# A mixture-of-experts tail: the last six prefetches of result rows are put behind the wait for all expert results

## The reference

```python
mod = (_silu(L0_c) @ L0_wmod).reshape(4, 6, 1, -1)
sa, ca, ga, sb, cb, gb = (mod[:, n] for n in range(6))   # ga, gb kept at least 0.25 away from zero
h = _layernorm(x) * (1 + ca) + sa
x = x + ga * attention(h)        # 16 heads, 4 sink keys and a window of 128 keys
h = _layernorm(x) * (1 + cb) + sb
x = x + gb * moe(h)
# moe: scores = sigmoid(h @ gate_w.T); the best 2 of 16 experts, their weights scaled to sum to 2.5
#   routed = sum over the two of weight * (silu(h @ w_gate[e]) * (h @ w_up[e])) @ w_down[e]
#   shared = (silu(h @ ws_gate) * (h @ ws_up)) @ ws_down
#   result = routed + shared
```

## Time and profile before

| | |
|---|---|
| time, median of 3 runs | 348.93 us (348.56 to 351.56) |
| span of the profiled execution | 347.5 us, first to last instruction |
| own time of the profiled execution | not listed apart; the median of the runs stands 1.43 us above its span |
| busy: PE / DVE / POOL / ACT | 80% / 67% / 59% / 47% of the span |
| DMA | 59.80 MB, mean 172 GB/s over the span |

### The profile page before, as it was taken

How to read it: one execution, slowest core, us unless ns; L and a number is a source line. 1 busy time by engine, 2 the same in 40 slices (tenths; PEclk the granted TensorE clock), 3 DMA queues, 4 the chain that set the end, 5 groups by cost and what they waited for, 6 DMA issues and landing times.

```text
span 347.5 us, 6287 instructions
## 1 busy us (share of the span) xinstructions
PE 278.8 (80%) x1665; PEld 215.0 (62%) x1666; DVE 231.3 (67%) x899; ACT 162.2 (47%) x518; POOL 205.2 (59%) x254
## 2 busy tenths in 40 slices
PE   4897889998988899989774999898899898886000
PEld 3264457656766576757543989787788787775000
DVE  0477477998889886997885645544345477763990
ACT  3142562278225822556222455454545566654550
POOL 3713116738784777558557356564655578875981
PEclk9996996999899996999988799999999999999555
DMA  7949001133624649702286644454456778869793
GB/s 261 330 132 347 16 2 49 59 100 115 197 80 135 183 127 320 163 30 93 72 228 205 201 138 121 144 177 133 138 160 180 245 210 254 263 188 343 247 360 139
DMA packets 41438, 59.80 MB, mean 172 GB/s; under 512 B 5092, under 2 KB 29880, under 8 KB 41404
## 3 DMA queue, kind: packets, MB, share of 16 engines
q1 hardware_dynamic: 34312, 39.91, 39.4%
q0 software_dynamic: 6528, 17.90, 14.3%
q10 hardware_dynamic: 564, 1.59, 1.4%
HBM read 33.57 MB, written 25.80 MB: 171 GB/s over the span
## 4 chain that ended last, share of the span: by engine, by line
PE 54%; DVE 22%; DMA 7%; issue 7%; ACT 4%; POOL 2%; another core or an unknown queue 1%; SPq 1%; DVEq 0%; POOLq 0%; ACTq 0%
PE bank L1227 16%; PE bank L892 8%; PE bank L1237 8%; PE bank L1085 6%; PE bank L1029 3%; PE bank L1052 3%; DVE bank L1752 3%; PE bank L1105 3%; DMA ht<-in_L_attn_x_dram 2%; PE bank L1067 2%; DVE h_sb L1369 2%; DMA ys<-pt_win,row_i 2%; PE bank L935 1%; PE bank L906 1%; DMA p_win<-slots 1%
## 5 line engine op out<-in xcount | busy, mean ns | idle before, releaser
L648 POOL DMA_INDIRECT ys<-pt_win,row_i x72 | 72.6, 1009 | 51.0 <-ACT pt_win L676 27.5
L1227 PE MATMUL bank<-ht,w_now 128*128 128x128 f32 x576 | 78.3, 280 | 4.4 <-issue 4.4
L593 POOL DMA_INDIRECT slots<-h_sb,slot_i x64 | 63.2, 987 | 30.1 <-issue 15.3
L1227 PEld LDWEIGHTS bank<-ht,w_now 128*128 128x128 f32 x576 | 71.7, 195 | 5.4 <-issue 5.1
L1741 DVE TENSOR_TENSOR act_t<-bank,sg 128x128 f32<-128x128 f32 x72 | 20.9, 290 | 48.5 <-ACT sg L843 33.2
L676 ACT ACTIVATE ht<-bank 128x256 f32<-128x256 f32 x104 | 39.9, 383 | 22.5 <-PE bank L892 15.6
L1237 PE MATMUL bank<-w_dn,act_t 128*128 x144 | 44.8, 393 | 5.4 <-DVE act_t L1741 4.3
L676 ACT ACTIVATE pt_win<-bank 128x256 f32<-128x256 f32 (+1 forms) x88 | 37.2, 423 | 21.7 <-PE bank L1237 9.6
L1085 PE MATMUL bank<-w_route,ht 128*128 128x272 f32 x128 | 41.5, 452 | 5.5 <-ACT ht L676 3.2
L892 PE MATMUL bank<-ident,p_win 128*128 128x128 f32 x198 | 36.1, 278 | 4.9 <-issue 3.2
L843 ACT ACTIVATE sg<-bank 128x128 f32<-128x128 f32 x72 | 20.1, 279 | 42.2 <-PE bank L1227 29.6
(11 more groups left out here) (260 smaller groups left out, 489.2 us busy)
## 6 DMA issues: line engine op xcount, KB each, us to landing
p_win<-slots SPq DMA_DIRECT2D x67, 129.0 KB
slots<-pads SPq DMA_DIRECT2D x28, 129.0 KB
xs<-in_L_attn_x_dram SPq DMA_DIRECT2D x3, 1024.0 KB
wmod_sb<-ys SPq DMA_DIRECT2D x12, 256.0 KB
w_gu<-ys SPq DMA_DIRECT2D x10, 256.0 KB, 2.8
mod_bc<-mod_rows_out SPq DMA_DIRECT2D x4, 512.0 KB, 5.7
w_dn<-in_L_ffn_w_down_dram SPq DMA_DIRECT2D x1, 2048.0 KB
h_sb<-ys SPq DMA_DIRECT2D x8, 256.0 KB
```

The source lines that it names most:

```text
L593: pool.indirect_dma_start(out=slots, out_offset=bass.IndirectOffsetOnAxis(ap=slot_i[:, k, j:j + 1], axis=0), in_=h_sb[:, j, :], in_offset= ...
L648: pool.indirect_dma_start(out=ys, out_offset=bass.IndirectOffsetOnAxis(ap=row_i[:, col:col + 1], axis=0), in_=y_sb[:, k, :], in_offset=Non ...
L1227: last = mm(bank[2 + k % 2][:, half * P:(half + 1) * P], w_now[:, k % 2, c, half * M:(half + 1) * M], ht[:, k, c, :], start=(c == 0), stop ...
```

## The change

On SP alone, after the loop of expert tiles: token loads 12 to 15 are issued as before; then SP waits for the landing of every put (and of every load of expert rows); then come token loads 16 to 21 without their own `half_done` waits, then the stores of token tiles 6 to 11, then token loads 22 to 31 and the remaining stores. `BEFORE_LAST` is 4 x GROUP = 16 token tiles.

```diff
         LAG = 2 * UNROLL
+        BEFORE_LAST = 4 * GROUP
...
-            for d in range(loaded, AHEAD * PAIR):
+            for d in range(loaded, BEFORE_LAST):
                 if d % GROUP == 0:
                     half_done(d // GROUP)
+                load_rows(d)
+            for k in range(UNROLL):
+                wait_apart(sp, y_out[k], fours * 16)
+                wait_apart(sp, xt_in[k], fours * 16)
+            for d in range(BEFORE_LAST, AHEAD * PAIR):
                 load_rows(d)
             for t in range(kept, loaded // GROUP * GROUP):
                 save(t, 1)
                 kept += 1
-            for k in range(UNROLL):
-                wait_apart(sp, y_out[k], fours * 16)
-                wait_apart(sp, xt_in[k], fours * 16)
             for d in range(AHEAD * PAIR, TILES):
                 load_rows(d)
```

## The result

The changed kernel is slower: the ratio to the kernel before is **1.0112, 95% interval 1.0064 to 1.0161**, about +3.9 us (2.2 to 5.6). Its median over four executions is 354.13 us; the kernel before, with a fourth execution, has 349.59. The profiled execution took 352.90 us with a span of 351.1. The forecast was 353.2 us and +4.3. A repeat beside the first experiments gave 1.0083 (1.0025 to 1.0141). All ratios leave out executions more than 1.5% above the fastest of the same kernel.

What follows compares the result with a forecast made beforehand. Put 67's late landing delays the weighing; VectorE's weighing and full DMA engines bound the last stage. Moved bytes +6.5 us, earlier stream start -2.2, so +4.3 on 348.93 gives 353.2 us, range 350.9 to 355.0.

Steps and rivals of the forecast that it cites:

- Put 67 is freed: End of expert tiles: with four loads ahead it lands about 317.2, copy of tile 71 about 318.85, put 71 gains 1.1 us.
- The rival that something else holds put 67: End of expert tiles: put 71 stays at 322.00, moved bytes cost in full, +5.4 us, time 354.3; chance 0.08.
- The wait: SP's queue after the first four loads: SP sits until put 71 has landed, so load 16 is issued at 323.6.
- The stall at tile 16: ScalarE in the weighing: tile 16 is taken at 327.2, 2.6 us later than now, after waiting for its loads.
- The sum's last step: Last stage: the stores' backlog ends later than the weighing, so the DMA engines decide the end; total +4.3 us.
- 5.5 us of ending: End of program: after the last transfers, 5.5 us follow whatever the kernel does, unchanged by the change.
- The first rival: Last stage: the weighing decides, not the transfers; weighing +3.4, transfers +2.9, time about 352.1; chance 0.23.
- The price of the moved bytes: Transfers behind the wait: six loads and six stores, 2.36 MB, cost 6.3 to 6.9 us, taken as 6.5.
- the second count: Weighing alone: tile 22 taken at 333.7, tile 31 at 341.9 against 338.55, +3.4 us.
- The rival of a gain: Last stage: the freed put's 1.8 us carries to the end, giving 347.1; chance 0.05.

Runs made afterwards that it cites:

- e7: e4 with the stores from token tile 6 on moved behind loads 22 to 31; ratio to the kernel before 0.9986 (0.9948 to 1.0024).
- e1: The changed kernel with the stores of token tiles 6 to 11 moved behind loads 22 to 31; ratio to the kernel before 1.0031 (0.9975 to 1.0086).
- e9: The kernel before with only the stores of tiles 6 to 11 moved behind loads 22 to 31; ratio to before 0.9995 (0.9951 to 1.0038).
- e4: The changed kernel, but loads 16 to 21 wait only for puts up to 67, the wait for all stands before load 22; ratio to before 1.0056.
- e10: e9 with one token load per expert tile from expert tile 58 on, five left for the end; ratio to the kernel before 1.0024 (0.9985 to 1.0062).
- e11: e9 with one token load per expert tile from expert tile 54 on, three left for the end; ratio to the kernel before 0.9978 (0.9943 to 1.0013).

## Why the prediction was right, and where it was not

The direction and the size were right: said +4.3 us, measured +3.9 (2.2 to 5.6) in time and +4.6 and +4.3 in two tails. The step from the transfers to the end was wrong, and that the size came out all the same is in part luck.

*Put 67 is freed: right.* Said: copy of tile 71 at once after TensorE, put 71 1.1 us earlier. Measured: +0.12, and 1.27 us earlier counted from TensorE's end. The rival that something else holds put 67 is out: with four loads ahead of it its packets had moved by 317, and in every kernel with eight or ten it released the copy only 6.0 to 6.3 us after its issue. What lets SP's packets go first, the runs don't show. The Trainium skill's rule that would have supported that rival ("DMA: Bandwidth & Descriptors", section "Queues, rings and completion order": each DMA engine takes turns between the queues, a packet of typically 9 to 17 descriptors, at most 64, at a time) fits badly, where 605 of SP's packets moved, about 38 to a DMA engine, and none of a put. A second stretch says less. In e7, from 324 to 326 us, with put 71 issued at 323.11, the two queues moved

```profile
q1 hardware_dynamic: 331, 0.61, 92.6%
q0 software_dynamic: 21, 0.06, 7.2%
```

which is one packet of a put to sixteen of SP's. If the profile counts SP's descriptors one by one, turns of that size would look like this; no run here shows what it counts.

*The wait: right.* Load 16 was issued at +4.48; said was 323.6, which is +4.8.

*The stall at tile 16: right.* Taken at +7.96, said 327.2, which is +8.4.

*The sum's last step: wrong.* "The stores' backlog ends later than that, so the DMA engines decide" is what failed, and with it the "5.5 us of ending" that "follow whatever the kernel does": in e1 the DMA engines stop 3.9 us before the end. For the transfers the sum was right: SP is through with its stores at 343.0 in the kernel before and at 346.4 in the changed one, +24.2 and +28.6, which is +4.4 where +4.3 was said (the stream grew by about 7.0 us, not 6.5, and started 2.55 us earlier, not 2.2). But the end doesn't hang on them. The first rival's mechanism, the weighing, sets the end, in this kernel and in all others tried, through POOL's DRAIN after it. e1 and e9 show it: in e1 the end comes 2.3 us earlier with the weighing while the transfers end 0.6 us earlier, and in e9 six more stores move in the last stage and the end stays. SP's row of 4.5 us for the others' ending was there to be read in the trace of before. That the transfers moved by 4.4 us and the weighing by 4.7 is a coincidence; it made the forecast of the time better than its reasoning.

*The price of the moved bytes: too low for the weighing.* For the loads a rate between 327 and 374 GB/s was taken, and 6.5 us for the six loads and six stores. Tile 16's loads released ScalarE at 325.75 and tile 22's at 334.01: 8.3 us, at about 250 GB/s for the first 5.5 us of the stream. So the weighing lost 4.7 us and not the 3.4 of the second count: it stood 0.4 us better than said at tile 16, and lost 1.8 us more than said on the way to tile 22.

*The rival of a gain* failed where it was said to: tile 16's loads were usable 4.3 us after ScalarE was free for them.

## What to carry to other kernels

A wait in the list that issues transfers holds everything written behind it: here 1.7 us were won at the front, and six loads and six stores lost their cover. When a transfer is held by others ahead of it, a later place for those can move the collision to the next transfer, as in e4 and e7. An earlier place took it away in e10 and e11, in the tail; in the time no gain was shown. And of two bounds that end close together, test which one is last by moving work off one of them only, and read what the last engine does at the end of the program: the DMA engines were full to 3.6 us after the last weighing and still had room, as SP was through with its stores 4.5 us before the end.

## What was not expected of the hardware

POOL's DRAIN at the end of the program took 7.7 us in each of the fourteen traces.

The first loads of a fresh stream were slow here. In the changed kernel the six loads and the start of the stores after the pause moved at 250 GB/s for 5.5 us with a DMA share of 0.85, and the ten loads after them at 368 with a share of 1.01, same shape and same source. In the kernel before, the first microsecond of the stream had 96 and the next seven 327. Whether the pause, the mixture with stores or the rows just written to `ys` makes this was not tried.
